# Layer 3 of a three-layer compressed interaction network: sums taken by ScalarE's accumulator in eight pieces, and a second chunk of one group split in two

## The reference, cut to what matters

```
B, M, D = (512, 32, 64)            # x0 is (B, M, D); three layers of 128 outputs
for i in range(3):
    H = h.shape[1]                 # 32, then 64, 64
    Wk = Ws[i].reshape(128, H, M)
    xk = relu(einsum('bhd,bmd,ohm->bod', h, x0, Wk) + bs[i][None, :, None])
    if i != 2:
        outs.append(xk[:, :64]); h = xk[:, 64:]
    else:
        outs.append(xk)
return concatenate([o.sum(axis=-1) for o in outs], axis=1)     # (B, 256)
```

## Time and profile before

| | |
|---|---|
| time of the profiled execution | 1762.16 us |
| its span, first to last instruction | 1760.4 us |
| median of three runs | 1762.63 us |
| DMA, mean over the span | 117 GB/s |
| granted clock of TensorE, mean | 0.994 |
| Vector engine, products into SBUF (L319), 128x2048 | 447 of 2283 ns |
| Vector engine, products into PSUM (L301), 128x2048 | 128 of 2290 ns |
| Vector engine, subtractions (L333), 128x2048 | 128 of 2281 ns |
| GpSimd, subtractions of 128x2048 (L414) | 318 of 4641 ns |
| TensorE, plain matmul instructions of layers 2 and 3 (L567) | 640 |
| TensorE, split matmuls of layers 2 and 3 (L574, L576, L583) | 1728 each |

### The profile page before, as it was taken

One profiled execution on the slowest core, in us unless ns is written; L12 is line 12 of the kernel. 1 busy time (PEld: TensorE's weight loads), 2 busy tenths in 40 slices (PEclk: granted clock), 3 DMA queues, 4 the chain that ended last, 5 costly groups with the idle time before them and its releaser, 6 DMA issues.

```text
span 1760.4 us, 19217 instructions
## 1 busy us (share of the span) xinstructions
PE 1737.2 (99%) x6734; PEld 1267.4 (72%) x6734; DVE 1679.4 (95%) x916; ACT 1307.8 (74%) x1222; POOL 1695.0 (96%) x451
## 2 busy tenths in 40 slices
PE   7899999999999999999999999999999999999998
PEld 4677777777777777777777777777777777777776
DVE  6999999999999999999999999999999999999996
ACT  4777777777777777777777777777777777777774
POOL 3899999999999999999999999999999999999997
PEclk8999999999999999999999999999999999999999
DMA  6324324324334233243343342332432433423410
GB/s 244 128 86 137 134 82 143 122 94 143 99 117 143 83 134 135 81 143 114 101 144 102 114 142 83 134 135 84 141 126 90 144 108 107 144 91 125 137 31 18
DMA packets 53424, 205.34 MB, mean 117 GB/s; under 512 B 10576, under 2 KB 11728, under 8 KB 45264
## 3 DMA queue, kind: packets, MB, share of 16 engines
q1 hardware_dynamic: 52976, 203.60, 34.7%
q10 hardware_dynamic: 352, 0.52, 0.1%
HBM read 153.75 MB, written 0.52 MB: 88 GB/s over the span
## 4 chain that ended last, share of the span: by engine, by line
PE 93%; ACT 2%; POOL 1%; issue 1%; DVE 1%; DMA 1%; ACTq 0%; SPq 0%; DVEq 0%; POOLq 0%
PE ACC L583 25%; PE ACC L576 25%; PE ACC L574 25%; PE ACC L567 15%; PE ACC L589 3%; ACT ZH L459 1%; POOL ZL L414 1%; DVE ZS L319 1%; DMA H<-H 0%; DMA W<-in_w 0%; DVE ZL L333 0%; ACT HP L442 0%; ACT WH L496 0%; DVE ZP L301 0%; DMA X<-in_xrows 0%
## 5 line engine op out<-in xcount | busy, mean ns | idle before, releaser
L414 POOL TENSOR_TENSOR ZL<-ZS,ZH 128x2048 fp32r<-128x2048 f32 (+1 forms) x446 | 1694.2, 3845 | 58.0 <-ACT ZH L459 57.4
L319 DVE TENSOR_TENSOR ZS<-HP,X 128x2048 f32<-128x2048 f32 x447 | 1009.7, 2283 | 51.3 <-issue 46.8
L459 ACT ACTIVATE ZH<-ZS 128x2048 fp32r<-128x2048 f32 (+1 forms) x446 | 707.1, 1599 | 12.9 <-DVE ZS L319 10.6
L574 PE MATMUL ACC<-ZH,WL 128*128 128x512 f32 x1728 | 539.3, 426 | 4.5 <-ACT R L487 2.7
L583 PE MATMUL ACC<-ZL,WH 128*128 128x512 f32 x1728 | 487.9, 396 | 8.1 <-POOL ZL L414 4.6
L576 PE MATMUL ACC<-ZH,WH 128*128 128x512 f32 x1728 | 487.3, 396 | 0.0
L442 ACT ACTIVATE HP<-H 128x512 f32<-128x512 f32 x256 | 152.6, 596 | 392.4 <-DVE ZS L319 287.7
L574 PEld LDWEIGHTS ACC<-ZH,WL 128*128 128x128 f32 x1728 | 325.0, 188 | 122.3 <-issue 35.0
L576 PEld LDWEIGHTS ACC<-ZH,WH 128*128 128x128 f32 x1728 | 325.2, 188 | 91.9 <-issue 15.3
L583 PEld LDWEIGHTS ACC<-ZL,WH 128*128 128x128 f32 x1728 | 324.4, 188 | 90.2 <-POOL ZL L414 7.9
L567 PE MATMUL ACC<-ZS,WF 128*128 128x512 f32 x640 | 295.3, 592 | 0.0
(11 more groups left out here) (37 smaller groups left out, 381.0 us busy)
## 6 DMA issues: line engine op xcount, KB each, us to landing
X<-in_xrows SPq DMA_DIRECT2D x62, 2048.0 KB, 7.5
H<-H SPq DMA_DIRECT2D x250, 128.0 KB, 2.3
XD<-in_xdup SPq DMA_DIRECT2D x64, 256.0 KB, 2.9
H<-H SPq DMA_DIRECT2D x252, 64.0 KB, 2.0
X<-in_xrows SPq DMA_DIRECT2D x3, 768.0 KB, 11.8
X<-in_xrows SPq DMA_DIRECT2D x1, 1280.0 KB, 9.2
X<-in_w SPq DMA_DIRECT2D x1, 896.0 KB, 10.8
X<-in_w SPq DMA_DIRECT2D x1, 832.0 KB, 14.7
```

Source lines behind the costliest of these rows:

```text
L319: nc.vector.tensor_tensor(ZS[:, m % PSLOTS, :, :], h, x, ALU.mult).then_inc(product_ready, 1)
L414: nc.gpsimd.tensor_tensor(ZL[:, n % LSLOTS, c, :], ZS[:, m % PSLOTS, c, :], ZH[:, n % HSLOTS, c, :], ALU.subtract).then_inc(low_by_pool, 1)
L459: nc.scalar.activation(ZH[:, n % HSLOTS, c, :], src, ACT.Copy).then_inc(high_ready, 1)
L574: nc.tensor.matmul(acc, wl[:, k, :], ZH[:, n % HSLOTS, c, :], start=(first and k == 0), stop=False)
```

## The change

Layer 3's third group keeps two plain chunks; its third chunk is split too (PARTS of layer 3 is 2 instead of 1), and both split chunks of this group, a new kind "half", no longer go through ZS and GpSimd but through ZP and the Vector engine, as in a vector group. The product of this group is then two instructions of 128 x 1024, the plain half into ZS and the split half into ZP. Because ZP is one buffer, low (i,2,0) moves ahead of product (i,2,2), and low (i,2,2) comes in the next iteration, behind `narrow` and ahead of product (i+1,1,0). Relu of layer 3 becomes eight activations of 128 x 64, written in place in ACC, each with an accumulator output into one column of `S3`; `sum3`, its semaphore and R3 go away (a buffer BLANK stands in for R3 in the opening matmuls), and the last transposes wait for the relu instead.

```diff
-PARTS = {1: 2, 2: 1}
+PARTS = {1: 2, 2: 2}
@@ kind
-    return ("vector", "pool", "mixed" if PARTS[layer] else "plain", "pool")[q]
+    return ("vector", "pool", "mixed" if layer == 1 else "half", "pool")[q]
@@ product
+                if kind(*g) == "half":
+                    whole, halved = slice(0, parts(*g).start), parts(*g)
+                    nc.vector.tensor_tensor(ZS[:, m % PSLOTS, whole, :], h_over(u, G - PARTS[layer]), x[:, whole, :],
+                                            ALU.mult).then_inc(product_ready, 1)
+                    dve.wait_ge(low_by_dve, VECTOR_NO[g])
+                    nc.vector.tensor_tensor(ZP[:, halved, :], h_over(u, PARTS[layer]), x[:, halved, :],
+                                            ALU.mult).then_inc(vector_ready, 1)
+                    return
@@ low
+                c = parts(i, layer, q)
+                nc.vector.tensor_tensor(ZL[:, n % LSLOTS, c, :], ZP[:, c, :], ZH[:, n % HSLOTS, c, :],
                                         ALU.subtract).then_inc(low_by_dve, 1)
@@ the Vector engine's loop
                 if live(i):
                     product(i, 0, 0)
                     narrow(i)
+                if live(i - 3) and i <= TILES + 1:
+                    low(i - 1, 2, 2)
...
                 if live(i - 2):
                     product(i, 2, 0)
                     product(i, 2, 1)
+                    low(i, 2, 0)
+                    product(i, 2, 2)
+                    product(i, 2, 3)
                     if i == TILES + 1:
-                        low(i, 2, 0)
-                    product(i, 2, 2)
-                    if live(i - 3):
-                        sum3(i - 3)
-                    if i <= TILES:
-                        low(i, 2, 0)
-                    product(i, 2, 3)
+                        low(i, 2, 2)
@@ relu on ScalarE
                 if layer == 2:
-                    if t >= 1:
-                        act.wait_ge(sums3, t)
-                    nc.scalar.activation(R3[:, :], acc[:, :], ACT.Relu, bias=b).then_inc(relu_done[2], 1)
+                    for n in range(BT):
+                        d = slice(D * n, D * n + D)
+                        last = nc.scalar.activation(acc[:, d], acc[:, d], ACT.Relu, bias=b,
+                                                    accum_out=S3[:, BT * t + n:BT * t + n + 1])
+                    last.then_inc(relu_done[2], 1)
                     return
@@ the end of TensorE's program
-            pe.wait_ge(sums3, TILES)
+            pe.wait_ge(relu_done[2], TILES)
+            pe.wait_ge(out12_ready, 1)
             turn3(BLOCKS - 1)
```

More of the change, by code:

```diff
@@ L49, in kind @@
         return "plain" if i < HEADS else "pool"
-    return ("vector", "pool", "mixed" if PARTS[layer] else "plain", "pool")[q]
+    return ("vector", "pool", "mixed" if layer == 1 else "half", "pool")[q]
 def parts(i, layer, q):
     k = kind(i, layer, q)
-    return slice(G, G) if k == "plain" else slice(G - PARTS[layer], G) if k == "mixed" else slice(0, G)
+    return slice(G, G) if k == "plain" else slice(G - PARTS[layer], G) if k in ("mixed", "half") else slice(0, G)
 def chunk_order(layer):
@@ L90, in numbered @@
     return {g: n for n, g in enumerate(g for g in GROUPS if kind(*g) in kinds)}
-POOL_NO, VECTOR_NO, PLAIN_NO = numbered("pool", "mixed"), numbered("vector"), numbered("plain", "mixed")
-SPLIT_NO, SLOT_NO = numbered("pool", "vector", "mixed"), numbered("pool", "plain", "mixed")
+POOL_NO, VECTOR_NO, PLAIN_NO = numbered("pool", "mixed"), numbered("vector", "half"), numbered("plain", "mixed", "half")
+SPLIT_NO, SLOT_NO = numbered("pool", "vector", "mixed", "half"), numbered("pool", "plain", "mixed", "half")
 SPLITS, SLOTTED = list(SPLIT_NO), list(SLOT_NO)
@@ L133, in cin_kernel @@
         R12 = sb("R12", [128, T])
-        R3 = sb("R3", [128, T])
+        BLANK = sb("BLANK", [128, T])
         S12 = sb("S12", [128, B + BT])
@@ L170, in cin_kernel @@
         relu_done = [sem(f"relu_done{n}") for n in range(3)]
-        sums12, sums3 = sem("sums12"), sem("sums3")
+        sums12 = sem("sums12")
         tr_done, tr12_done = sem("tr_done"), sem("tr12_done")
@@ L177, in wait_low @@
         def wait_low(engine, g):
-            if kind(*g) == "vector":
+            if kind(*g) in ("vector", "half"):
                 engine.wait_ge(low_by_dve, VECTOR_NO[g] + 1)
@@ L316, in product @@
                         dve.wait_ge(plain_used, PLAIN_NO[before] + 1)
-                    if kind(*before) != "plain":
+                    if kind(*before) in ("pool", "mixed"):
                         dve.wait_ge(low_by_pool, POOL_NO[before] + 1)
+                if kind(*g) == "half":
[6 more added lines that the diff above has]
+                    return
                 nc.vector.tensor_tensor(ZS[:, m % PSLOTS, :, :], h, x, ALU.mult).then_inc(product_ready, 1)
@@ L332, in low @@
                 dve.wait_ge(high_ready, n + 1)
-                nc.vector.tensor_tensor(ZL[:, n % LSLOTS, :, :], ZP[:, :, :], ZH[:, n % HSLOTS, :, :],
+                c = parts(i, layer, q)
+                nc.vector.tensor_tensor(ZL[:, n % LSLOTS, c, :], ZP[:, c, :], ZH[:, n % HSLOTS, c, :],
                                         ALU.subtract).then_inc(low_by_dve, 1)
@@ L343, in sum12 @@
                                      R12[lo:hi, :].rearrange("p (b d) -> p b d", d=D), AX.X).then_inc(sums12, 1)
[L345 to L348, removed]
             def gather12(n):
@@ L401, in _ @@
             gather12(BLOCKS - 1)
-            sum3(TILES - 1)
             gather3(BLOCKS - 1)
@@ L406, in _ @@
         def _(pool):
-            nc.gpsimd.memset(R3[:, :], 0.0).then_inc(blank, 1)
+            nc.gpsimd.memset(BLANK[:, :], 0.0).then_inc(blank, 1)
             for g in POOL_NO:
@@ L607, in group @@
                 g = i, layer, q
-                if kind(*g) in ("plain", "mixed"):
+                if kind(*g) in ("plain", "mixed", "half"):
                     plain(g, acc, WF[layer], range(parts(*g).start), False)
@@ L628, in keep_warm @@
                 for _ in range(count):
-                    nc.tensor.matmul(acc, R3[:, 0:OUT], R3[:, :], start=True, stop=True)
+                    nc.tensor.matmul(acc, BLANK[:, 0:OUT], BLANK[:, :], start=True, stop=True)
             pe.wait_ge(blank, 1)
@@ L649, in _ @@
                             pe.wait_ge(sums12, TILES + 1)
-                            pe.wait_ge(sums3, 128 * (BLOCKS - 1) // BT)
+                            pe.wait_ge(relu_done[2], 128 * (BLOCKS - 1) // BT)
                             for n in range(BLOCKS - 1):
```

## The result

The changed kernel takes 1984.86 us (median of 4 runs, 1979.42 to 1989.02), the kernel before 1762.82 us in the same comparison: a ratio of 1.126, with a 95% interval of 1.123 to 1.129. The forecast was 1973 us. The profiled execution took 1979.42 us, with a span of 1977.5 us.

What follows compares the result with a forecast made beforehand. A loop of waits over ScalarE and the Vector engine bounds it: 26.98 + 3.2 = 30.2 us, 3.37 more an iteration. Over 62 iterations 209 us, plus 2 at the end, on 1762.16 gives 1973 us; range 1872 to 2035.

Steps and rivals of the forecast that it cites:

- The loop: ScalarE 13.88 us, Vector engine 12.90 from low (i,2,0) on, hand-overs 0.2: 26.98 + X us per iteration.
- X: ScalarE's time for the eight relu pieces of layer 3: 3.2 us, 0.40 a piece; lower end 1.71, upper 5.0.
- The second path to low (i,2,0): After relu, TensorE needs 5.6 us to free the slot of (i,1,1), ScalarE 6.6 us: ScalarE later by 1 us.
- the falling clock as a rival: TensorE idles over 3 us an iteration, the granted clock falls, TensorE is the bound at 33.3 us: 2165 us, chance 0.03.
- What the profile was to show: Vector engine idle ahead of low (i,2,0) by ScalarE, 2 us or more; TensorE near 88%; pieces some 0.4 us.
- The Vector engine without room: Vector engine's work rises from 26.06 to 26.68 us an iteration, just what TensorE needs; any new wait counts in full.
- Faster by 10 us: Rival: waits on the Vector engine are absorbed, TensorE stays the bound with 0.16 us less an iteration: 1752 us, chance 0.08.

Runs made afterwards that it cites:

- the kernel with the half group in ZS: Changed kernel, half group's product whole into ZS and read there, low (i,2,0) behind product (i,2,2) again: 1784.82 us, ratio 1.0125.
- The experiment with the zeros: Changed kernel plus two float32 matmuls of zeros in TensorE's idle time ahead of layer 1's low part: 1937.55 us, ratio 1.099.
- the ZS half first: Changed kernel with the ZS half of product (i,2,2) moved ahead of low (i,2,0): 1876.06 us, ratio 1.065.
- low (i-1,2,2) out of the loop: The kernel with the half group in ZS, this low moved from behind `narrow` to behind product (i,1,0): 1937.00 us, ratio 1.099.

## Why the prediction was right, and where it was not

**The loop.** Right. It gave 26.98 + X us. With the measured X of 2.33 it is 29.31; the iterations without a fall of the clock take 29.55. Most of the 0.24 us more lies at one hand-over that I had left out: product (i+1,1,0) overwrites ZP, so it waits for low (i,2,2) and starts 1.32 us behind it (1009.46 to 1010.78) where I had counted 1.14. In the kernel with the half group in ZS this low reads ZS, the distance is 1.13 us, and the period, 27.08, is within 0.05 us of the sum. Moving one half out of the loop, filling TensorE's idle time and freeing ZP each changed the period by about what the loop says.

**X.** The step that was mis-sized. I took 3.2 us, by 0.40 us a piece; it is 2.33, by 0.29. That there is one more instruction a piece was right, its price was not: I counted its fixed 0.186 us in full, and it overlaps its neighbours. By X alone the sum would have been 1762 + 62 x 2.48 + 1 = 1917 us, and 2.33 us is at the lowest edge of the 2.3 to 4.2 us to which I gave 0.57. The estimate by the Trainium skill's page "ScalarE: Activation LUTs", section "What ACT_TABLE_LOAD costs", 0.240 us a piece, has no reading of the sum in it; the trace has 0.22 from the start of the first piece to its reading (1020.53 to 1020.75).

**The second path to low (i,2,0).** The step that failed. I wrote that TensorE needs 5.6 us for (i,1,0) and (i,1,1), so that ScalarE is the later by 1 us. Two things were wrong in it. At full clock the margin is 0.56 us and not 1: TensorE starts 0.20 us after the relu ends, which I had left out, and takes 5.85 us to its last end. And TensorE needed 7.4 us, from 1023.06 to 1030.47, in the iteration shown, in which its clock fell behind an idle time of 2.0 us, and was itself the later in 50 of 63 waits. The experiment with the zeros prices this at 47 us. I had the falling clock as a rival with 0.03, but priced it as a bound of TensorE's whole work, 2165 us, and not as a delay on a path that stood 1 us from the end. So that 1973 us came close is in part luck, by errors of opposite sign: some 55 us too much for X, 47 us too little for the clock and 62 x 0.24 = 15 us too little for the hand-over. Put right, the sum is 1979 us, 6 us below the median of 1984.86. The same sum without the clock is 1932 us for the run with the zeros, which took 1937.55: some 6 us are left open in both. That the profiled execution took 1979.42 us is chance; it was the shortest of the four.

**What the profile was to show.** Shown: the idle time ahead of the low and none ahead of the products, ScalarE without a wait ahead of its copy, and TensorE far from 99% (92% against the forecast 88%; slow matmuls are longer). Not shown: ScalarE as the releaser in most iterations, and the pieces of 0.4 us.

**The Vector engine without room.** Right as arithmetic: it has 26.86 us of work in the iteration of 30.51 that idles for 3.65, against my 26.68; the 0.18 us are the same hand-over.

**Faster by 10 us.** It did not come in any order tried. To reach it, the second chunk's low would, as I read the runs, have to leave ScalarE's loop without a second input in SBUF. A second ZP buffer might do that, but ZP is already four of the kernel's eight PSUM tiles of 128x512, and more was not tried.

## What to carry to other kernels

When an engine has no room left, ask of each instruction that moves forward whether its input is ready there; a single buffer that forces an order can close a loop of waits whose length is the sum over several engines, and no busy share shows it. Add up that loop, and every path to its last wait, at both levels of TensorE's clock: a path that is 0.5 us short of the end at full clock may set it when the clock falls near an idle gap. And before moving an instruction to cut a loop, list all that it waits for, slots included, and what runs on GpSimd at its new place.

## What the runs showed that I had not expected

- An activation with an accumulator output is followed by an instruction of its own, 216 ns by its mean, which costs only some 0.08 us in distance: 0.29 us for 64 elements and their sum.
- In the changed kernel TensorE idled once an iteration for 2.0 to 2.8 us, and in 50 of 61 iterations the granted clock fell to 1.2 GHz, mostly for 3.4 us (mean clock 0.952). The fall began anywhere from 1.1 us before work resumed to 1.6 us after. With a gap of 0.9 us (the zeros) there was no such fall (mean 0.996), with 1.6 us (the ZS half first) there were 5 (0.992). The length of the gap alone doesn't decide: with low (i-1,2,2) out of the loop TensorE idled for 2.3 us in some 40 iterations, and the clock fell 20 times (0.977).
- A subtraction on the Vector engine with both inputs in SBUF of 128x1024 took 1.22 us where it met GpSimd's instructions for less than 0.1 us, and 4.3 us on the mean where it began while one was under way.
